# First stage as a pipeline over its 32 tiles, with centred weights, row sums from a column of ones, one chain for three norms, and keys spread by GpSimd

## What is computed

```python
nw = N // WINDOW                              # windows of 64 tokens, 16 heads of 8
qkv = (xw @ W_qkv).reshape(B * nw, WINDOW, 3, NUM_HEADS, HEAD_DIM)
q = _layernorm(q, ln_gamma, ln_beta)          # over the 8 features of a head
k = _layernorm(k, ln_gamma, ln_beta)
attn = softmax(einsum('bqhd,bkhd->bhqk', q * SCALE, k))     # SCALE = 1
out = einsum('bhqk,bkhd->bqhd', attn, v) @ W_proj + b_proj
```

## Time and profile before

| | us |
|---|---|
| median of three runs | 3812.87 |
| their range | 3811.61 to 3819.72 |
| profiled execution, its own time | 3801.54 |
| its span, from the first to the last instruction | 3799.7 |
| busy: TensorE, VectorE, ScalarE, GpSimd | 3233.2, 3009.8, 2600.9, 2503.0 |
| mean granted clock of TensorE, as a share of full | 0.933 |

### The profile page before, as it was taken

One profiled execution on the slowest core, in us unless ns is written; L12 is line 12 of the kernel. 1 busy time (PEld: TensorE's weight loads), 2 busy tenths in 40 slices (PEclk: granted clock), 3 DMA queues, 4 the chain that ended last, 5 costly groups with the idle time before them and its releaser, 6 DMA issues.

```text
span 3799.7 us, 126632 instructions
## 1 busy us (share of the span) xinstructions
PE 3233.2 (85%) x52674; PEld 2775.9 (73%) x52674; DVE 3009.8 (79%) x4462; ACT 2600.9 (68%) x3787; POOL 2503.0 (66%) x2289
## 2 busy tenths in 40 slices
PE   3444447999989999989999899999899998999996
PEld 2333236788878888778888788888788887888885
DVE  5766767888888788888788887888887888888883
ACT  2222235777777778778787777787687777788775
POOL 1000007887777778778787777887787787788772
PEclk8666668999999999999999999999999999999997
DMA  1000001111111111111111111111111111111111
GB/s 57 0 0 0 0 0 35 37 55 33 33 34 39 57 35 36 36 35 38 57 36 35 30 41 59 36 35 36 34 38 53 36 36 35 37 37 40 30 35 32
DMA packets 54638, 129.97 MB, mean 34 GB/s; under 512 B 10944, under 2 KB 28864, under 8 KB 53312
## 3 DMA queue, kind: packets, MB, share of 16 engines
q1 hardware_dynamic: 54080, 122.02, 11.0%
HBM read 19.25 MB, written 2.10 MB: 6 GB/s over the span
## 4 chain that ended last, share of the span: by engine, by line
PE 56%; DVE 17%; issue 11%; ACT 11%; POOL 5%; DMA 0%; SPq 0%; POOLq 0%; ACTq 0%; DVEq 0%
PE pair L214 44%; PE pair L217 12%; ACT qT L736 6%; POOL qk L959 3%; DVE ss L860 2%; DVE ts L856 2%; DVE pair L873 1%; DVE den L908 1%; ACT sq L726 1%; DVE qk L852 1%; ACT sq L718 1%; POOL Sx L991 1%; DVE qT L359 1%; DVE mx L877 1%; DVE VA L344 0%
## 5 line engine op out<-in xcount | busy, mean ns | idle before, releaser
L980 POOL TENSOR_TENSOR qk<-qk,ts 128x1024 f32<-128x1024 f32 x384 | 910.9, 2383 | 218.8 <-DVE ts L856 205.0
L959 POOL TENSOR_TENSOR qk<-qk,rn 128x1024 f32<-128x1024 f32 x384 | 734.0, 1932 | 43.6 <-issue 28.8
L852 DVE TENSOR_TENSOR qk<-pair,tab 128x1024 f32<-128x1024 f32 x384 | 468.7, 1221 | 370.3 <-ACT sq L718 368.2
L214 PE MATMUL pair<-wq_h,xs_h 128*128 128x512 f32 x1154 | 515.7, 447 | 36.5 <-issue 18.6
L217 PE MATMUL pair<-small,qk 128*128 128x128 f32 x3192 | 452.4, 285 | 79.0 <-ACT qT L736 40.4
L217 PEld LDWEIGHTS pair<-small,qk 128*128 128x128 f32 x3192 | 360.2, 145 | 168.4 <-issue 96.0
L991 POOL TENSOR_TENSOR Sx<-Sx,rden 128x1024 f32<-128x1024 f32 x192 | 365.7, 1905 | 157.3 <-DVE rden L911 157.3
L856 DVE TENSOR_TENSOR ts<-pair,tab 128x1024 f32<-128x1024 f32 x384 | 466.7, 1215 | 0.0
L214 PE MATMUL pair<-wq_h,xs_l 128*128 128x512 f32 x1152 | 465.0, 404 | 0.0
L860 DVE TENSOR_REDUCE ss<-sq 128x16 f32<-128x1024 f32 x384 | 464.6, 1210 | 0.0
L713 ACT ACTIVATE Sx<-Sx 128x1024 f32<-128x1024 f32 x192 | 203.7, 1061 | 378.0 <-DVE Sx L881 378.0
(11 more groups left out here) (201 smaller groups left out, 7079.4 us busy)
## 6 DMA issues: line engine op xcount, KB each, us to landing
VB<-VA SPq DMA_DIRECT2D x192, 384.0 KB, 3.5
VB<-VA SPq DMA_DIRECT2D x96, 128.0 KB, 3.5
wq_raw<-wqkv SPq DMA_DIRECT2D x6, 1536.0 KB, 8.4
xf<-xT SPq DMA_DIRECT2D x96, 64.0 KB, 1.9
xf<-xT SPq DMA_DIRECT2D x96, 63.8 KB, 2.0
wo_sb<-wo SPq DMA_DIRECT2D x6, 512.0 KB, 3.7
out<-X SPq DMA_DIRECT2D x8, 256.0 KB, 2.3
...
```

What stands on the lines that cost most here:

```text
L214: return T_.matmul(out, lhsT, rhs, start=start, stop=stop, **k)
L852: V_.tensor_tensor(h3(qk[:, now, kind, :], DH), h3(source[:, :], DH), rep(tab[:, 2 * kind, b, :], HEADS, DH), ALU.mult)
L959: G_.tensor_tensor(x, x, bc(rn[:, then, kind * HEADS:(kind + 1) * HEADS], HEADS, DH), ALU.mult).then_inc(S["scaled"], 1)
L980: G_.tensor_tensor(qk[:, now, kind, :], qk[:, now, kind, :], ts[:, kind, :], ALU.add).then_inc(S["added"], 1)
```

## The change

The loop over four lanes is replaced by a pipeline that is written out over 42 steps. In step s each engine works on several tiles at different depths: tile s+1 has its statistics taken, s is normalised, s-1 is projected, s-2 has q and k scaled, s-3 has them transposed and its keys spread, s-4 has scores and Exp, s-5 is transposed and weighs the values, s-6 is divided and projected, s-7 gets its residual, s-8 its second norm, s-9 is stored. Each event has its own semaphore, and `nth` gives the count to wait for. Within the new functions the order of the instructions on an engine is the order of the text. In detail:

- The weights of q and k are centred once over each head (`wc`, in `prepare`), so the products come out centred; head sums, means and centring are gone.
- Each head of the values gets a ninth column that holds one (`v1`), so the weighing of values gives the row sums too; the sums on VectorE are gone. The values of odd heads are written in the rows of the second half, of even heads in the first, with zeros elsewhere, by two copies of ScalarE; the product with the parity mask is gone.
- The three inverse roots of a step (tile s, the heads of s-2, tile s-8 again) lie side by side in 34 columns and take one Ln, one Exp and four operations on GpSimd.
- Gamma and beta are applied by the copies of transposed k and q (`scale`, `bias` of the activation).
- Keys are spread by GpSimd, as 8 heads on 64 rows each: 128x512 a window instead of 128x1024. The scores then contract 64 rows.
- The bias is added to x by GpSimd early, and the residual adds the projection to it.
- x is loaded in four parts with a semaphore each. The table products, the rounding and the split of the layer weights move into steps 3 to 8.

In the diff below eight leading blanks are cut from each line. "..." stands for what is left out: views of scratch buffers, and waits for the reuse of a buffer by an earlier tile. The removed functions are those printed above.

```diff
@@ consts, tensors, semaphores @@
-    head_mask = (np.arange(P)[:, None] // DH1 == np.arange(H1)[None, :])
-    parity = (np.arange(P)[:, None] // W1N == (np.arange(P)[None, :] // DH1) % 2)
+    own_head = (np.arange(P)[:, None] % W1N // DH1 == np.arange(H1 // 2)[None, :])
...
@@ stage @@
+HALF1 = H1 // 2
...
+NN = 2 * H1 + 2
+V_RING = 6
...
+B_S, B_PT, B_IN, B_OUT = PB, PA1, banks[6], banks[7]
...
+def qkv_b(i):
+    return banks[i % 2]
+def nth(name, i, k=None):
+    return FIRST[name] * i + (FIRST[name] if k is None else k)
+def tile(i):
+    return 0 <= i < TILES
+def norm(s):
+    return 0 <= s < TILES + 8
+def first_stage(e, step):
+    for s in range(-1, TILES + 9):
+        step(e, s)
+def prepare(dve):
+    V_.memset(st[:, 0:336], 1.0)
+    V_.memset(v1[:, :, :, :], 0.0).then_inc(S["v_zeroed"], 1)
+    dve.wait_ge(S["v_zeroed"], 1)
+    ones = v1[:, :, :, :].rearrange("p r w (n d) -> p r w n d", d=2 * NV)
+    for r in range(V_RING):
+        V_.memset(ones[0:W1N, r, :, :, DH1], 1.0)
+        last = V_.memset(ones[W1N:P, r, :, :, NV + DH1], 1.0)
+    last.then_inc(S["v_cleared"], 1)
+    dve.wait_ge(S["w_loaded"], 16)
+    V_.tensor_reduce(w_mean, h3(w_qkv[:, 0:2 * P], DH1), axis=AX.X, op=ALU.add).then_inc(S["w_summed"], 1)
+    dve.wait_ge(S["w_summed"], 1)
+    V_.tensor_scalar(w_mean, w_mean, 1.0 / DH1, None, ALU.mult).then_inc(S["w_meant"], 1)
+    dve.wait_ge(S["w_meant"], 1)
+    V_.tensor_tensor(h3(wc, DH1), h3(w_qkv[:, 0:2 * P], DH1), bc(w_mean, 2 * H1, DH1), ALU.subtract).then_inc(S["w_centred"], 1)
+    dve.wait_ge(S["v_cleared"], 1)
+def first_dve(e, s):
+    i = s - 7
+    if tile(i):
+        e.wait_ge(S["a_biased"], nth("a_biased", i))
+        e.wait_ge(S["a_y_done"], nth("a_y_done", i))
+        if tile(i + 1):
+            e.wait_ge(S["a_pv_done"], nth("a_pv_done", i + 1))
+        V_.tensor_tensor(X1[:, i, :], y_b, X1[:, i, :], ALU.add).then_inc(S["a_resid"], 1)
+    if norm(s - 1):
+        e.wait_ge(S["a_eps"], nth("a_eps", s - 1))
+    i = s - 2
+    if tile(i):
+        e.wait_ge(S["a_squared"], nth("a_squared", i))
+        V_.tensor_reduce(ss1, h3(sq1, DH1), axis=AX.X, op=ALU.add).then_inc(S["a_summed"], 1)
+    i = s - 7
+    if tile(i):
+        e.wait_ge(S["a_resid"], nth("a_resid", i))
...
+        V_.bn_stats(st6b, X1[:, i, :]).then_inc(S["a_stats2"], 1)
+        e.wait_ge(S["a_stats2"], nth("a_stats2", i))
...
+        V_.bn_aggr(mv1[:, (s + 1) % 2, 1, :], st6b).then_inc(S["a_aggr2"], 1)
+    i = s - 4
+    if tile(i):
+        e.wait_ge(S["a_scored"], nth("a_scored", i))
+        if tile(i - 1):
+            e.wait_ge(S["a_shifted"], nth("a_shifted", i - 1))
+        V_.tensor_reduce(mx1, h3(B_S[:, :], W1N), axis=AX.X, op=ALU.max).then_inc(S["a_maxed"], 1)
+    i = s - 6
+    if tile(i):
+        e.wait_ge(S["a_pv_done"], nth("a_pv_done", i))
...
+        V_.reciprocal(rden1, o_b[:, :, DH1]).then_inc(S["a_inverse"], 1)
+        e.wait_ge(S["a_inverse"], nth("a_inverse", i))
...
+        V_.tensor_tensor(h3(o1, DH1), o_b[:, :, 0:DH1], bc(rden1, H1, DH1), ALU.mult).then_inc(S["a_divided"], 1)
+    i = s - 4
+    if tile(i):
+        e.wait_ge(S["a_maxed"], nth("a_maxed", i))
...
+        V_.tensor_tensor(h3(sx1[:, i % 2, :], W1N), h3(B_S[:, :], W1N), bc(mx1, H1, W1N),
+                         ALU.subtract).then_inc(S["a_shifted"], 1)
+    i = s + 1
+    if tile(i):
+        if i % 8 == 0:
+            e.wait_ge(S[f"x_in{i // 8}"], 16)
...
+        V_.bn_stats(st6, X1[:, i, :]).then_inc(S["a_stats"], 1)
+        e.wait_ge(S["a_stats"], nth("a_stats", i))
...
+        V_.bn_aggr(mv1[:, i % 2, 0, :], st6).then_inc(S["a_aggr"], 1)
+    if norm(s):
+        e.wait_ge(S["a_normed"], nth("a_normed", s))
+    i = s
+    if tile(i):
...
+        V_.tensor_scalar(xn[:, i % 2, :], X1[:, i, :], mv1[:, s % 2, 0, 0:1], rn1[:, s % 2, 2 * H1:2 * H1 + 1],
+                         ALU.subtract, ALU.mult).then_inc(S["a_xn"], 1)
+    i = s - 2
+    if tile(i):
+        e.wait_ge(S["a_v_kept"], nth("a_v_kept", i))
...
+        V_.tensor_tensor(h3(qkn[:, i % 2, :], DH1), h3(qkv_b(i)[:, 0:2 * P], DH1), bc(rn1[:, s % 2, 0:2 * H1], 2 * H1, DH1),
+                         ALU.mult).then_inc(S["a_qkn"], 1)
+    i = s - 8
+    if tile(i):
...
+        V_.tensor_scalar(z1[:, i % 2, :], X1[:, i, :], mv1[:, s % 2, 1, 0:1], rn1[:, s % 2, 2 * H1 + 1:2 * H1 + 2],
+                         ALU.subtract, ALU.mult).then_inc(S["a_z"], 1)
+def first_pool(e, s):
+    if norm(s):
+        if tile(s - 2):
+            e.wait_ge(S["a_summed"], nth("a_summed", s - 2))
+        if tile(s):
+            e.wait_ge(S["a_aggr"], nth("a_aggr", s))
+        if tile(s - 8):
+            e.wait_ge(S["a_aggr2"], nth("a_aggr2", s - 8))
...
+        G_.tensor_scalar(var1[:, 0:2 * H1], ss1, LN_EPS, None, ALU.add).then_inc(S["a_eps"], 1)
+        G_.tensor_scalar(var1[:, 2 * H1:NN], mv1[:, s % 2, :, 1], LN_EPS, None, ALU.add).then_inc(S["a_eps"], 1)
+    i = s - 1
+    if tile(i):
+        e.wait_ge(S["a_xn"], nth("a_xn", i))
+        G_.tensor_tensor(X1[:, i, :], X1[:, i, :], bias_out, ALU.add).then_inc(S["a_biased"], 1)
+    if norm(s):
+        e.wait_ge(S["a_seed"], nth("a_seed", s))
+        G_.tensor_tensor(nt1, var1, y1, ALU.mult).then_inc(S["a_newton"], 1)
+        e.wait_ge(S["a_newton"], nth("a_newton", s, 1))
+        G_.tensor_tensor(nt1, nt1, y1, ALU.mult).then_inc(S["a_newton"], 1)
+        e.wait_ge(S["a_newton"], nth("a_newton", s, 2))
+        G_.tensor_scalar(nt1, nt1, -0.5, 1.5, ALU.mult, ALU.add).then_inc(S["a_newton"], 1)
+        e.wait_ge(S["a_newton"], nth("a_newton", s, 3))
...
+        G_.tensor_tensor(rn1[:, s % 2, 0:NN], nt1, y1, ALU.mult).then_inc(S["a_normed"], 1)
+    i = s - 3
+    if tile(i):
+        e.wait_ge(S["a_k_kept"], nth("a_k_kept", i))
...
         for w in range(2):
+            last = G_.tensor_tensor(h3(kx1[:, i % 2, w * UNIT:(w + 1) * UNIT], W1N),
+                                    rep(kT1[:, w * W1N:(w + 1) * W1N], HALF1, W1N), bc(own_head, HALF1, W1N), ALU.mult)
+        last.then_inc(S["a_spread"], 1)
+    if 4 <= s < 7:
+        rest_of_projection(e, Place(e, 0).at(0), 0, s - 4, G_.tensor_tensor)
+    if s == 8:
+        e.wait_ge(S["rot_loaded"], 16)
+        tables(e, Place(e, 0).at(0), 0, G_.tensor_tensor)
+def first_act(e, s):
+    i = s - 1
+    if tile(i):
+        e.wait_ge(S["a_xT_done"], nth("a_xT_done", i))
...
+        A_.activation(xnT[:, i % 2, :], xnT_b, ACT.Copy).then_inc(S["a_xT_kept"], 1)
+    if norm(s):
+        e.wait_ge(S["a_eps"], nth("a_eps", s))
...
+        A_.activation(ln1, var1, ACT.Ln, scale=LN_IN_SCALE).then_inc(S["a_ln"], 1)
+        e.wait_ge(S["a_ln"], nth("a_ln", s))
...
+        A_.activation(y1, ln1, ACT.Exp, scale=-0.5, bias=vec_half[:, 0:1]).then_inc(S["a_seed"], 1)
+    i = s - 5
+    if tile(i):
+        e.wait_ge(S["a_pT_done"], nth("a_pT_done", i))
...
+        A_.activation(pT1, B_PT[:, :], ACT.Copy).then_inc(S["a_pT_kept"], 1)
+    i = s - 3
+    if tile(i):
+        e.wait_ge(S["a_qkT_done"], nth("a_qkT_done", i))
+        if tile(i - 1):
+            e.wait_ge(S["a_spread"], nth("a_spread", i - 1))
+        A_.activation(kT1, qkT_b[:, P:2 * P], ACT.Identity, scale=gamma, bias=beta).then_inc(S["a_k_kept"], 1)
...
+        A_.activation(qT1[:, i % 2, :], qkT_b[:, 0:P], ACT.Identity, scale=gamma, bias=beta).then_inc(S["a_q_kept"], 1)
+    i = s - 6
+    if tile(i):
+        e.wait_ge(S["a_oT_done"], nth("a_oT_done", i))
...
+        A_.activation(oT1, oT_b, ACT.Copy).then_inc(S["a_oT_kept"], 1)
+    i = s - 4
+    if tile(i):
+        e.wait_ge(S["a_shifted"], nth("a_shifted", i))
+        A_.activation(sx1[:, i % 2, :], sx1[:, i % 2, :], ACT.Exp).then_inc(S["a_exp"], 1)
+    i = s - 1
+    if tile(i):
+        e.wait_ge(S["a_qkv_done"], nth("a_qkv_done", i))
...
+        A_.activation(sq1, qkv_b(i)[:, 0:2 * P], ACT.Square, scale=float(DH1) ** -0.5).then_inc(S["a_squared"], 1)
...
+        for odd in range(2):
+            rows = slice(odd * W1N, (odd + 1) * W1N)
+            new = qkv_b(i)[rows, 2 * P:4 * P].rearrange("p (w n h d) -> p w n h d", w=2, h=2, d=DH1)[:, :, :, odd, :]
+            to = v1[rows, i % V_RING, :, :].rearrange("p w (n h d) -> p w n h d", h=2, d=NV)[:, :, :, odd, 0:DH1]
+            A_.activation(to, new, ACT.Copy).then_inc(S["a_v_kept"], 1)
+    i = s - 9
+    if tile(i):
+        e.wait_ge(S["a_zT_done"], nth("a_zT_done", i))
+        A_.activation(xT[:, i * P:(i + 1) * P], zT_b, ACT.Copy).then_inc(S["a_zT_kept"], 1)
+    if 3 <= s < 6:
+        e.wait_ge(S["wq_loaded"], 16)
+        round_projection(s - 3)
+def first_pe(e, s):
+    i = s - 4
+    if tile(i):
+        e.wait_ge(S["a_spread"], nth("a_spread", i))
+        e.wait_ge(S["a_q_kept"], nth("a_q_kept", i))
+        if tile(i - 1):
+            e.wait_ge(S["a_shifted"], nth("a_shifted", i - 1))
         for w in range(2):
             for half in range(2):
+                rows = slice(half * W1N, (half + 1) * W1N)
```

(63 more changed lines are left out.)

367 lines of the change are left out of this document (125 added, 242 removed).

## The result

The changed kernel takes 3448.8 us (median of four runs, 3445.4 to 3455.0) against 3812.2 of the kernel before beside it: 0.905 of its time, with a 95% interval of 0.902 to 0.908.

The account below looks back on a forecast made before the run. The first stage was taken as bound by its order, the layers by unchanged work; 6.5 + 16 + 195.2 + 14.5 + 4 = 236.2 us instead of 568.8 gives 3468.9, plus 11.3 to the median: 3480 us, range 3452 to 3547.

Parts of the forecast that it names:

- What bounds the kernel; 13.8 to 568.8 can be saved: First stage, 13.8 to 568.8 us: bound by its order, with no engine full, so the time to save lies there.
- The step, 6.1: One full step of the new first stage: 6.1 us, 32 of them 195.2 us.
- The ring I named: Path through a step: scores, transpose, copy, norm, pT, kT, spread, next scores; 5.9 us.
- The 0.2 for three near-ties: Pipeline step: 0.2 us added to 5.9 because three queues come within 0.5 us and each waits for the others.
- kT at 0.28: ScalarE's copy of transposed k in a step: 0.28 us, with gamma and beta riding on it at nothing.
- TensorE 0.45 before the next scores: TensorE's queue in a step: weighed values end at 5.45 us, 0.45 before the next scores.
- Scores side by side, 1.05: Scores on TensorE: products on the array's two halves run side by side, 1.05 us to the last result; otherwise 1.92.
- Start and ramps: Stage's edges: start 6.5 us, steps 0 to 3 16 us, steps 36 to 40 14.5 us.
- moved work: Steps 4 to 8: layer-weight splits and table products moved there delay the norm and pT, 4 us.
- The shared port: Rival: VectorE's SBUF normalisations wait for GpSimd's spread, losing up to 2.1 us a step; 3500 to 3547 us; chance 0.09.
- The layers unchanged at 3231: Layers behind the first stage: keep their 3230.9 us; if not, the forecast fails by that difference.
- 11.3 from the execution to the median: Whole kernel: median of three timed runs, 3812.9, lies 11.3 us above the profiled execution; added to 3468.9.

Follow-up runs that it names:

- late_scores: Changed kernel with a tile's scores and all that stands behind them one step later; step 5.74 us, execution 3450.7 us.
- division_first: Changed kernel with reciprocal and division ahead of the maximum on VectorE; step 5.81 us, execution 3442.6 us.
- half_spread: Changed kernel with GpSimd spreading the keys of the first window only, so the output differs; step 5.74 us, execution 3434.4 us.
- both_rings: Changed kernel with scores one step later, division ahead of the maximum and the spread first in GpSimd's step; 3453.6 us, ratio 0.909.
- the repeat: Changed kernel, unchanged, profiled a second time; 3449.8 us, ratio 0.906 to the kernel before.
- The shifts: Unused transposes ahead of TensorE's stage: 24 or 12 in the kernel before (timed 3794.5 and 3794.7 against 3798.9 us), 24 in the changed kernel (layers 3207.5).

## Why the prediction was off, point by point

- *What bounds the kernel; 13.8 to 568.8 can be saved:* right. The stage fell by 342, and the clock in its steps rose to 1.00.
- *The step, 6.1:* 5.81, and this is the stage's largest term, 9.3 us. The ring I named was the one that set the step, and its walk gave 5.9 bare; the spread took 1.04 a half, not 1.09. The 0.2 for three near-ties was not there: `late_scores` and `division_first` show rings of 5.81 and 5.74 side by side with no surcharge.
- *Small slips in the sums:* four statistics in 1.03 give an overlap of 0.04 between neighbours and not 0.08; the 5.2 agrees with 0.04 for each of the 13 instructions. The loads in proportion give 5.2 and not 5.1. ScalarE works at 76% of the layers and not at 77. None moves the forecast by more than 0.2 us.
- *kT at 0.28, since gamma and beta ride "at nothing":* wrong by a little. The copy with a scale and a bias lasts 0.45, but it starts 0.10 before pT's end, so the path kept its length.
- *TensorE 0.45 before the next scores:* wrong. My walk had the output projection at 4.1 and the values' end at 5.45; they stand at 4.38 and 5.81, with the products of v and the transpose of z between. It cost nothing here, but it hid the second ring: `half_spread` gained 0.07 instead of 0.4.
- *Scores side by side, 1.05:* right, 1.09. *Start and ramps:* 37.0 forecast, 35.0 measured; *moved work* 4 and 5.7.
- *The shared port:* its mechanism is real, its place wrong. The two normalisations lose 0.16 and 0.40 a step, within the "up to 2.1", and it cost the step next to nothing: `half_spread` gave the 0.40 back and the step fell by 0.07. It takes part in the limit in `both_rings`. I had argued that nothing shows the form in a mode that takes both ports, as it lasts 342 ns: that inference failed. The normalisation waits for the end of GpSimd's instruction, as the rows above show. The Trainium skill (SBUF — State Buffer, Who interferes with whom) lets such a mode and GpSimd exclude each other, and the trace agrees in that (0.74 beside the spread, 0.33 without). The Trainium skill (VectorE: DVE Perf Modes, The perf-mode tier table) gives that mode the double rate, which no run here shows.
- *The layers unchanged at 3231:* the step that failed, and the largest single miss. I took a stretch whose instructions the change leaves alone to keep its 3230.9 us; it took 3217.0 and, in the repeat, 3218.9. I had named it as what would make the forecast fail, and gave it no width in the range. The shifts show that moving TensorE's code moves its stops; most of the size stays open.
- *11.3 from the execution to the median:* taken from three runs whose median lay high; it was 3.4 after, and five groups of 4 to 23 runs of before have medians from 3798.9 to 3812.2. With these two, of 14 and 8 us, the time fell 3 us under the range's lower end, though the stage itself (226.6) lies well within the 207 to 265 I had given it; either of the two alone would have left it inside. The range let the step vary and nothing else.
